# A decoder layer on one core: the router's norm statistics made in the cross-attention's loop, its matrix held in the array, two tiles' norms and the W1 split placed later in the opening

## The reference

```python
x = x + _L0_attn_ref(_layernorm(x), ...)      # 8 layers of linear attention and a hidden layer of 1024
x = x + _L0_xattn_ref(_layernorm(x), ctx_512, ctx_512, ...)   # 16 heads of 16, context 128 x 128 per sequence
x = x + _L0_ffn_ref(_layernorm(x), gate_w, ...)

def _layernorm(x, axis=-1, eps=1e-05):
    m = jnp.mean(x, axis=axis, keepdims=True)
    v = jnp.var(x, axis=axis, keepdims=True)
    return (x - m) / jnp.sqrt(v + eps)

# in _L0_ffn_ref: each token goes to one of 8 experts, and all go to a shared one
shared_out = _swiglu(x, shared_gate, shared_up, shared_down)
logits = x @ gate_w.T                         # 2048 tokens x 8 experts
top_id = jnp.argmax(logits, axis=-1)
score = jax.nn.sigmoid(jnp.max(logits, axis=-1))
xs = x * score[:, None]
# routed_out: for each expert, _swiglu of the rows of xs whose top_id it is
return shared_out + routed_out
```

## Time and profile before

| | before |
|---|---|
| median of 3 runs | 2961.05 us (2959.04 to 2965.14) |
| the profiled execution's own time | 2964.72 us |
| its span, first to last instruction | 2962.1 us |
| PE busy | 2821.0 us, 95% |
| DVE busy | 2419.0 us, 82% |
| ACT busy | 1919.5 us, 65% |
| POOL busy | 778.5 us, 26% |
| mean granted TensorE clock | 0.977 |
| attention stack (to its last matmul's wait, about) | 0 to 2483 us |
| cross-attention | 2483 to 2711 us |
| router, up to `down(0)` | 2711 to 2761 us |
| rest of the shared expert | 2761 to 2827 us |
| routed experts | 2828 to 2962 us |

### The profile page before, as it was taken

One profiled execution on the slowest core, in us unless ns is written; L12 is line 12 of the kernel. 1 busy time (PEld: TensorE's weight loads), 2 busy tenths in 40 slices (PEclk: granted clock), 3 DMA queues, 4 the chain that ended last, 5 costly groups with the idle time before them and its releaser, 6 DMA issues. The chain is left out here.

```text
span 2962.1 us, 35837 instructions
## 1 busy us (share of the span) xinstructions
PE 2821.0 (95%) x13034; PEld 2337.4 (79%) x13034; DVE 2419.0 (82%) x3599; ACT 1919.5 (65%) x2849; POOL 778.5 (26%) x513
## 2 busy tenths in 40 slices
PE   5799999999999999999999999999999996997989
PEld 4688888888888888888888888888888874776777
DVE  7878898889888988898889888988898855774366
ACT  5667777777777777777777777777777742443155
POOL 4003231223122312231223122312331124331313
PEclk9899999999999999999999999999999997996999
DMA  4000001000100010001000100010100014100122
GB/s 141 1 1 22 29 12 36 22 24 17 36 22 22 18 36 22 22 19 36 22 22 19 36 17 27 19 36 11 33 18 20 1 57 161 74 0 0 50 44 36
DMA packets 62469, 91.88 MB, mean 31 GB/s; under 512 B 16480, under 2 KB 42336, under 8 KB 60256
## 3 DMA queue, kind: packets, MB, share of 16 engines
q1 hardware_dynamic: 58224, 85.46, 9.2%
q0 software_dynamic: 4080, 4.27, 0.8%
HBM read 80.24 MB, written 10.38 MB: 31 GB/s over the span
## 5 line engine op out<-in xcount | busy, mean ns | idle before, releaser
L407 PE MATMUL PS<-XTHI,WHI 128*128 128x512 f32 x1536 | 624.8, 407 | 24.4 <-DVE EX L733 18.8
L409 PE MATMUL PS<-XTHI,WLO 128*128 128x512 f32 x1536 | 608.3, 396 | 0.0
L408 PE MATMUL PS<-XTLO,WHI 128*128 128x512 f32 x1536 | 604.3, 393 | 0.0
L618 ACT ACTIVATE ATT<-INV,CC,CE 128x128 f32<-128x128 f32 x1024 | 432.4, 484 | 122.7 <-PE Y L449 116.4
L449 PE MATMUL Y<-WO,ATT 128*128 128x256 f32 x2048 | 454.6, 380 | 6.6 <-ACT ATT L618 6.6
L449 PE MATMUL Y<-W2S,H 128*128 128x256 f32 x2048 | 457.5, 379 | 2.3 <-DVE T L805 1.4
L449 PEld LDWEIGHTS Y<-WO,ATT 128*128 128x128 f32 x2048 | 389.7, 190 | 63.3 <-ACT ATT L618 6.2
L449 PEld LDWEIGHTS Y<-W2S,H 128*128 128x128 f32 x2048 | 386.2, 190 | 56.4 <-DVE T L805 1.8
L323 POOL TENSOR_TENSOR RSTD<-MV,EPS 128x4 f32<-128x4 f32 x68 | 16.1, 238 | 1348.7 <-DVE MV L820 1339.3
L407 PEld LDWEIGHTS PS<-XTHI,WHI 128*128 128x128 f32 x1536 | 291.7, 190 | 90.3 <-issue 21.5
L583 ACT ACTIVATE EX<-PS,BNEG 128x512 f32<-128x512 f32 x256 | 165.8, 685 | 299.1 <-DVE INV L785 156.3
(11 more groups left out here) (201 smaller groups left out, 4881.3 us busy)
## 6 DMA issues: line engine op xcount, KB each, us to landing
STAGE<-L_attn_Wkvq SPq DMA_DIRECT2D x64, 384.0 KB, 3.2
WO<-L_attn_Wo SPq DMA_DIRECT2D x8, 1024.0 KB, 4.8
W2S<-L_attn_W SPq DMA_DIRECT2D x8, 1024.0 KB, 4.7
STAGE<-L_attn_W SPq DMA_DIRECT2D x32, 256.0 KB, 5.5
WGU<-L_ffn_r_gate SPq DMA_DIRECT2D x8, 512.0 KB, 8.8
WGU<-L_ffn_r_up SPq DMA_DIRECT2D x8, 512.0 KB, 8.6
WD<-L_ffn_r_down SPq DMA_DIRECT2D x8, 512.0 KB, 8.8
rows_in<-ZERO SPq DMA_DIRECT2D x1, 3036.0 KB, 16.7
```

Source lines behind the costliest of these rows:

```text
L407: nc.tensor.matmul(out, whi[:, kc, :], xhi[:, kc, :], start=(kc == 0), stop=False)
L408: nc.tensor.matmul(out, whi[:, kc, :], xlo[:, kc, :], start=False, stop=False)
L409: ins = nc.tensor.matmul(out, wlo[:, kc, :], xhi[:, kc, :], start=False, stop=(kc == KD - 1))
L618: ins = nc.scalar.activation(ATT[:, 2 * p + i, ss], INV[:, b, i, ss], ACT.Identity, scale=CE[:, b, k:k + 1], bias=CC[:, b, k:k + 1])
```

## The change

**Opening.** `norm_input(2)` and `norm_input(3)` leave the first tile's loop over pairs and stand in `slot(0, 0)`, ahead of the `newton` of the last pair and ahead of the `newton` of the next tile's first pair. POOL waits for `recip` to reach 4, that is for the first tile's last `newton`, before it splits W1. **Cross-attention.** The context arrives transposed (the host lays it out so, as one more of the layouts in `packed`), so that CSEQ's copy, its transpose and ACT's copy go; the loops are written out over 16 sequences; each sequence's statistics are taken two instructions after its `shifted` of the next, and POOL makes the first 12 sequences' powers at the end of its list, the last four in the router. **Router.** The gate (GT, 8 columns) is the stationary matrix and 512 columns of ZG stream through it; the logits come out as 8 rows, ACT copies them to LT, and PE transposes them back, four transposes for a tile. The last tile's stand behind `gate_up(0, 0)`, and ACT makes `high(0)` after tile 0's logits and `high(1)` after tile 3's.

```diff
-        sp.dma_start(self.CTXS, ctx_in.rearrange("b s d -> s b d")).then_inc(self.x_in, 16)
+        sp.dma_start(self.CTXS, ctx_in).then_inc(self.x_in, 16)
...
+    def router_rstd(self, nc, pool, half, bs, k):
+
+        pool.wait_ge(self.mv, bs.stop)
+        nc.gpsimd.tensor_scalar(self.RSTD[:, bs], self.MV[:, bs, 1], 1e-5, None, ALU.add).then_inc(self.v0, 1)
+        pool.wait_ge(self.v0, 4 + k)
+        nc.gpsimd.tensor_tensor(self.RSTD[:, bs], self.RSTD[:, bs], half[:, bs], ALU.pow).then_inc(self.r0, 1)
...
+            pool.wait_ge(recip, PAIRS)
             for k in range(HC, PIECES):
                 split_hidden(0, k, True)
...
+                opening = type(l) is int and g == 0
+                if opening:
+                    norm_input(2)
                 if tile:
                     newton(tl, tt, 3)
...
                     denominators(nl, nt, 0)
+                    if opening:
+                        norm_input(3)
                     newton(nl, nt, 0)
...
-                if p < TILES - 1:
-                    norm_input(p + 1)
                 if p == 0:
+                    norm_input(1)
                     newton(0, 0, p)
...
         def steps(engine, run):
-            for j in range(2):
-                run(0, j)
-            with engine.Fori(1, SEQS // 2 - 1, 1) as i:
+            for i in range(SEQS // 2):
                 for j in range(2):
                     run(i, j)
-            for j in range(2):
-                run(SEQS // 2 - 1, j)
...
-                nc.tensor.transpose(A[:, 2 * P:3 * P], CSEQ[:, j, :], ident[:, :]).then_inc(zct_mm, 1)
...
-                nc.scalar.copy(CT[:, j, :], A[:, 2 * P:3 * P]).then_inc(zct, 1)
...
-                nc.vector.tensor_copy(CSEQ[:, j, :], CTXS[:, b, :])
...
+            def statistics(b):
+
+                dve.wait_ge(upd, b + 1)
+                nc.vector.bn_stats(ST[:, b, :], X[:, b, :]).then_inc(st, 1)
+                dve.wait_ge(st, b + 1)
+                nc.vector.bn_aggr(MV[:, b, :], ST[:, b, :]).then_inc(cross.mv, 1)
...
                 if after:
                     shifted(b + 1, 0)
+                if before:
+                    statistics(b - 1)
                 output(b, j, 1)
...
             def logits(q):
                 pe.wait_ge(zg, q + 1)
-                for b in range(TS):
-                    s = q * TS + b
-                    for kc in range(KD):
-                        ins = nc.tensor.matmul(PSX[:, 6, s * E:(s + 1) * E], ZG[:, q, kc, b * P:(b + 1) * P],
-                                               GT[:, kc, :], start=(kc == 0), stop=(kc == KD - 1))
-                return ins
+                if q >= 2:
+                    pe.wait_ge(lt, q - 1)
+                for kc in range(KD):
+                    ins = nc.tensor.matmul(PSX[0:E, q % 2, :], GT[:, kc, :], ZG[:, q, kc, :], start=(kc == 0),
+                                           stop=(kc == KD - 1))
+                ins.then_inc(lt_mm, 1)
+
+            def turn_logits(q):
+                pe.wait_ge(lt, q + 1)
+                for b in range(TS):
+                    s = q * TS + b
+                    ins = nc.tensor.transpose(PSX[:, 6, s * E:(s + 1) * E], LT[:, q % 2, b * P:(b + 1) * P],
+                                              ident[0:E, 0:E])
+                ins.then_inc(lg_mm, 1)
...
             for q in range(TILES):
                 turn_rows(q)
+                if q > 1:
+                    turn_logits(q - 2)
                 if q > 0:
                     logits(q - 1)
-            logits(TILES - 1).then_inc(lg_mm, 1)
+            turn_logits(TILES - 2)
+            logits(TILES - 1)
             gate_up(0, 0)
+            turn_logits(TILES - 1)
             gate_up(0, 1)
             counts()
...
-            for b in range(SEQS):
-                ins = nc.vector.bn_stats(ST[:, b, :], X[:, b, :])
-            ins.then_inc(prep, 1)
-            dve.wait_ge(prep, 1)
-            for b in range(SEQS):
-                ins = nc.vector.bn_aggr(MV[:, b, :], ST[:, b, :])
-            ins.then_inc(prep, 1)
-            dve.wait_ge(r0, 1)
-            dve.wait_ge(prep, 2)
             for q in range(TILES):
+                if q == 0:
+                    dve.wait_ge(cross.r0, 4)
+                if q == TILES - 1:
+                    dve.wait_ge(cross.r0, 5)
```

75 lines of the change are left out of this document (45 added, 30 removed).

## The result

The changed kernel took 2940.41 us (median of four runs, 2937.52 to 2944.48), the kernel before 2960.67 us beside it (2959.04 to 2965.14). The ratio is 0.9930, with a 95% interval of 0.9916 to 0.9944: 20.3 us or 0.7% faster. Forecast were 2941 us and a gain of 20.4 us. In another set of runs the same kernel took 2940.71 us, the ratio to before being 0.9937 (0.9924 to 0.9951).

What follows compares the result with a forecast made beforehand. Bounds: DVE in the opening, PE in the cross-attention, a DVE-POOL-DVE-PE chain at low clock in the router. 5.4 + 1.0 + 14.0 = 20.4 us off the median 2961.05 gave 2940.7, given as 2941; range 2933 to 2952.

Steps and rivals of the forecast that it cites:

- The opening, 5.4 us: Opening: moving two norms and POOL's W1 split off DVE's path gains 5.5 us, less 0.1 us reaching PE.
- Its two intermediate times: Opening, DVE: features of pair 2 start at 54.5 us, those of pair 3 at 66.8.
- The rival that the split's cost is only moved: Opening: DVE loses 3.7 us or more beside tile 1's first pair; 2944.4 to 2946.1 us; chance 0.14.
- The cross-attention, 1.0 us: Cross-attention: 0.5 us won at the entry and 0.5 by written-out loops; transpose and in-loop statistics costed at nothing.
- the written-out loops save register work, 0 to 1 us in all, taken as 0.5: Cross-attention: register work ahead of some DVE instructions goes, 0.5 us won.
- The 0.5 us for the context at the entry: Cross-attention entry: only there are the context's transpose and copies a chain, so dropping them wins 0.5 us.
- The router, 14.0 us: Router: an earlier first transpose and a higher PE clock bring `down(0)` from 2761.16 to 2747.1, 14.0 us won.
- forecast 11.8 - 2.8 = 9.0: Router: PE's first transpose, 11.8 us behind the last update before, now comes at 2714.1 instead of 2723.08.
- I take it that tile 0's logits raise it: Router, PE: tile 0's 512-column logits raise the clock from 1.2 GHz; the other 16.2 us of work halve to 8.1.
- 16.4: Router, PE: time from first transpose to shared expert, 15.6 us plus 0.8 for a later clock rise.
- from TOTS to `down(0)` DVE's list is what it was, 8.93 us: Router's end: DVE's work between TOTS and the first `down` keeps its length, 8.93 us.
- What follows runs as it did: From the first `down` to the kernel's end: no time won or lost.

Runs made afterwards that it cites:

- The halves: Two kernels, each the changed kernel with part of its opening undone: W1 split early again, 2943.12 us; norms of tiles 2 and 3 at their old place, 2938.79 us.
- the second trace: Profile of the changed kernel run once more, unedited, in another set of runs: 2940.71 us (2938.63 to 2945.37, 5 runs).

## Why the prediction was right, and which of its steps were not

**The opening, 5.4 us: right.** Its two intermediate times were met within 0.2 us, the gaps took the norms, and the tensor_scalars beside the moved split lost 1.3 us (forecast 1.7). 5.8 us were won at the first slot and at PE's first hidden matmul, 3.7 at the stack's end in this pair of traces, about 5 over all. The halves show what I had not separated: of 5.7 us, 2.8 come from the coincidence of norm and split, so that either edit alone wins most of them (the late split 4.8, the late norms 3.8). The norm's own share is 1.0 us, not 1.3. The rival that the split's cost is only moved fell. The Trainium skill (SBUF — State Buffer, "SBUF: two separate sides") has GpSimd and some forms of DVE work block one another instead of sharing the port. The traces agree on the block (the norm takes 4.80 us beside the split and 1.38 alone); in the new place it cost 1.3 us, since only the two tensor_scalars lost time there.

**The cross-attention, 1.0 us: the mechanism right, both sizes too small.** The step "the written-out loops save register work, 0 to 1 us in all, taken as 0.5" failed in its size: 1.7 us go with the loops. The 0.5 us for the context at the entry are 1.0 us. Together that is 2.7 us; in this pair of traces the low-clock stretches take 0.3 of them back. The transpose was rightly costed at nothing, and the statistics in the loop cost nothing, as forecast. What the loops' extra time consists of, register work or other, no run shows.

**The router, 14.0 us: 13.2 us in this pair of traces, by terms that erred in both directions.** The early statistics brought 9.4 us (forecast 11.8 - 2.8 = 9.0). The step "I take it that tile 0's logits raise it" failed as a cause: the clock was up ahead of the logits in this trace, and rose with the old logits too. In its place the runs show that it did not stay up with the 8-column form. In time this made the start of the shared expert 14.5 us behind the first transpose (15.2 in the second trace), not 16.4. The step "from TOTS to `down(0)` DVE's list is what it was, 8.93 us" failed by 3.2 us. The list is the same, but it met POOL's multiplication, which before had ended 1.1 us into the additions. The profile of before held the clue: POOL's multiplication, 9.32 us long, starts when ACT's sigmoid is done, and the sigmoid waits for the logits, which are now read behind the shared expert's first piece. So it started 1.2 us behind that piece's first matmul before and starts 4.4 us behind it now (2726.73 behind 2722.31), while TOTS comes 7.5 us behind it instead of 9.0. I asked what covers the statistics and the norms, but not what stands beside DVE's additions. This is the port rule once more, at a place where I had not asked it: with POOL behind them, or done, the additions take 3.2 to 3.4 us.

**"What follows runs as it did": wrong by 2.8 us, in the kernel's favour.** It was 200.9 us and is 198.1 (197.2 in the second trace), though the first `down` now takes 1.6 us more at the low clock. The kernel before lost this in its own waits beside the scatter, 7.15 us on DVE (remote) and 3.91 on PE ahead of its second `down`, which its trace shows and I took as given. The run without the scatter shows that such waits need it. The old logits alone bring them back (202.7 us), so in this kernel more of the new logits' worth lies here than ahead of `down`, where they bring 0.2 to 0.9 us with the early statistics (37.9 against 37.0 and 37.7 us) and 3.3 without them (50.3 against 47.0). Why the logits' form decides on waits so far behind them is not shown.

**The sum.** In spans 3.7 + 2.4 + 13.2 + 2.8 = 22.1 us, and 20.3 in the medians. Against this pair of traces the forecast was too low by 1.4 us in the cross-attention and by 2.8 behind `down`, too high by 1.7 in the opening and by 0.8 in the router. That it met the median within 1 us is luck: four terms were off, in both directions, and single executions of one kernel lie further apart than that.

## What to carry to other kernels

When an edit moves an engine's work earlier, look not only at what waits for it but at what it will now run beside: 16 additions of 128x8 on DVE cost 3.2 us alone and 6.8 beside a multiplication on POOL, and a norm 1.4 or 4.8. Independent arithmetic between two pieces of a pipeline (here the routing between tile 0's gates) belongs behind the pieces, if the engine is idle there anyway: that was worth 6.3 us, a third of the whole change, for moving a few lines. And a change of three parts deserves three experiments, read by the distance between two instructions and not by the total: two of its edits, the norms' place and the context's layout, are worth 1.0 us each, which no median here shows.

## What the runs showed of the hardware that I had not expected

- TensorE's granted clock fell from 2.4 to 1.2 GHz in the middle of work without a gap, with transposes and 8-column matmuls only (0.91 in 2714 to 2717, 0.50 behind it, one trace), and stayed up in the same place with 512-column matmuls between the transposes, in twelve traces.
- During an indirect scatter of 16 row blocks, issued one each 1.27 us, ACT and DVE can stand still for 4 to 16 us with no releaser in the trace, and PE for 3.6 to 4.1 us behind them. Without the scatter they don't. With the same scatter at another place of the program they didn't either. What decides it was not found.
- Writing out the hardware loops (six passes of two sequences on PE, ACT and DVE, seven on POOL) saved 1.7 us, 0.3 us a pass (25.44 us instead of 25.14), although PE set the pace.
